# Swin blocks on one core: the subtraction of row maxima as four 32-row products, behind the four biases

## The chip, the cores and the metric

The kernel runs on one core of a Trainium2 chip. Time is that of the device, in microseconds (us), from the start of the program to its end; a profiled execution also gives its span, from the first to the last instruction. Lower is better. The engines are named as the profile names them: PE (TensorE, matmuls), PEld (its weight loads), DVE (VectorE), ACT (ScalarE), POOL (GpSimd), SP (SyncE, which issues most DMAs).

## What is computed

The input is 16 images of 28x28 pixels with 64 channels. Two Swin blocks are applied (the second with windows shifted by 3 and a mask), then a whitening of the channels in groups of 16. What the change touches is the attention in each 7x7 window, for 8 heads of 8 channels:

```
wins = y.reshape(Bn, Hh // WS, WS, Ww // WS, WS, Cc)          # windows of 49 tokens
wins = wins.transpose(0, 1, 3, 2, 4, 5).reshape(-1, N, Cc)
qkv = (wins @ qkv_w + qkv_b).reshape(-1, N, 3, HEADS, hd).transpose(2, 0, 3, 1, 4)
q, k, v = (qkv[0], qkv[1], qkv[2])
attn = jnp.einsum('whnd,whmd->whnm', q, k) * hd ** (-0.5)
attn = attn + bias[None]
attn = attn.reshape(Bn, NW, HEADS, N, N) + mask[None, :, None]
attn = jax.nn.softmax(attn.reshape(-1, HEADS, N, N), axis=-1)
out = jnp.einsum('whnm,whmd->whnd', attn, v)
```

## The kernel before

**Tiling.** An image pair (one image in partitions 0 to 63, one in 64 to 127) is cut into two items of 392 tokens, 8 windows each. A block has 16 items (`HALVES`), and the loop over them is software-pipelined by hand: each engine has its own `step(...)`, written out in the order in which it is to run, and semaphores tie the engines together. Around the two loops of 16 steps stand a start (input, weights, tables), an MLP part behind each block, and the whitening at the end.

**Scores twice.** The softmax needs the row maximum of each query, but the exponential is taken on transposed scores (keys in partitions), where a row maximum lies along partitions. So PE computes the scores of an item twice. `scores` (line 1070) writes them with queries in partitions: a bias product per bank (`bn`), then the products `kexp,qsb`. DVE takes the maxima from there (`rowmax`, line 808, negated, into `nmax`). `split_max` multiplies them by a mask for even and odd windows (`nmaxw`), `maxt` on PE turns them (50 columns, 128 rows in PSUM: one row per combination of window and head), and `spread_max` on DVE writes `rx`, in which each of these 128 rows stands at the columns of its own window and head half only (constant `slot`). One item later `scores_t` (line 1085) writes the transposed scores. They lie in four PSUM banks (`SC`, one bank for each head number h4 = 0..3 within a half), and each of the two groups (`grp`, four windows) fills all four banks: for each bank a bias product (`bt`, 117 rows), then a product of `rx` with a selector (`sel_r`, 128 rows) that adds the negated maximum of the right head to every key; then the products `qexp,ksb`, 16 of 32 rows and 49 columns, each of which the profile counts as two instructions. All in F32R or F32. ACT takes the exponential of two banks at a time (`expo`, line 531), `pv` multiplies with the values, and the row sums go through DRAM to be inverted and spread (`dpk`, `rpk`, `dens`, `rec`).

**Order on PE in a step G** (line 1123 on): `scores_t(G, 0)`, `pv(G-1, 1)`, `f_v`, `scores(G+1, 0)`, two centring products (`xh`, `xl`), `proj(G-2)`, `scores(G+1, 1)`, variance and `f_qk` (`wk`, `wq`) of later items, `scores_t(G, 1)`, `maxt(G+1)`, `pv(G, 0)`.

**What frees the banks.** All score products share the four banks. Before its bias, a group waits for the engine that last read banks 0 and 1, and before the third bias for banks 2 and 3: ACT's exponential (`exp_done`) in the first group of a step, DVE's maxima (`max_done`) in the second. The first group also waits for `rx` (`rx_done`), ahead of everything.

**DVE in a step**: the reciprocals of item G-1, between them the maxima of `scores(G+1, 0)`, the residual, the maxima of `scores(G+1, 1)`, `split_max`, then a chain of eight small operations (`root`, lines 787 to 796, an inverse square root), in the middle of which `spread_max` stands.

**SP in a step**: `dpk` of the second half, `dens` and `rec` of both halves, four transfers `kexp`, four `qexp` for item G+2, and `dpk` of the first half of G, in this order in one queue.

**Start.** ACT's queue loads constants, weights and, as the last large one, the selector `sel` (`sel_f` lies in the memory of `hid`), while SP's queue loads the images. DVE rounds `sel_f` to `sel_r`.

Of the kernel before, what the change touches and what calls it, by code (L numbers as in the profile page):

```python
# [5 lines left out]
F32R = mybir.dt.float32r  # L6
I32 = mybir.dt.int32
ACT = mybir.ActivationFunctionType
ALU = mybir.AluOpType
AX = mybir.AxisListType  # L10

IMAGES, SIDE, CH, HEADS, WS, SHIFT = 16, 28, 64, 8, 7, 3
HD = CH // HEADS
NTOK = WS * WS
# [3 lines left out]
WIN = 2 * WROW  # L18
TOK = WIN * NTOK
IMG_TOK = SIDE * SIDE  # L20
KROWS = 64 + NTOK
# [19 lines left out]
TILES4 = 4  # L41
GWIN = WIN // 2
BANK = GWIN * 2 * NTOK
# [17 lines left out]
def build(nc, x, par, gamma, beta, con, out):  # L61

    ctx = ExitStack()
    with ctx:
        def sb(name, shape, dt=F32):
            return ctx.enter_context(nc.sbuf_tensor(name, shape, dt))
# [30 lines left out]
        wmask = con_view("wmask", KROWS)  # L97
        slot = con_view("slot")
# [8 lines left out]
        hidb = sb("hid", [128, 4, TOK])  # L107

        hid = [hidb[:].rearrange("p (c r) n -> p c r n", c=2), ptb[:, 0].rearrange("p (c r) n -> p c r n", c=2)]
        sel_f = hidb[:].rearrange("p a b -> p (a b)")[:, 0:WIN * 128]  # L110
        sel_r = sb("sel_r", [128, WIN, 128], F32R)


        G1, B1, G2, B2, QB, KB, VB, PB, F2B, FB = 0, 1, 2, 3, 4, 5, 6, 7, 8, 9
# [31 lines left out]
        qsb = sb("qsb", [128, TOK])  # L146
        ksb = [sb(f"ksb{i}", [128, TOK]) for i in range(3)]
        vbd = [sb(f"vbd{i}", [KROWS, WIN * HEADS, 32]) for i in range(2)]
        nmax = sb("nmax", [KROWS, WIN, HEADS])
        nmaxw = sb("nmaxw", [KROWS, WIN // 2, 2, 2 * HEADS], F32R)  # L150
        rx = sb("rx", [128, 2 * GWIN, NTOK], F32R)
        pt = [ptb[0:KROWS, i] for i in range(2)]
        osb = [sb(f"osb{i}", [128, 4 * NROWS]) for i in range(2)]
# [36 lines left out]
        SC = psum[:, 0:TILES4]  # L190
# [485 lines left out]
        def _(dve):  # L676
# [131 lines left out]
            def rowmax(g1, grp):  # L808
                dve.wait_ge(s_ready, 2 * g1 + grp + 1)
                for b in (0, 2):  # L810
                    nc.vector.tensor_reduce(  # L811
                        nmax[:, GWIN * grp:GWIN * grp + GWIN, :].rearrange("p w (g a) -> p a w g", g=2)[:, b:b + 2],
                        SC[0:KROWS, b:b + 2, 0:BANK].rearrange("p a (w g m) -> p a w g m", w=GWIN, g=2),
                        AX.X, ALU.max, negate=True).then_inc(max_done, 1)

            def split_max(g1):

                dve.wait_ge(max_done, 4 * (g1 + 1))
                dve.wait_ge(mxt_ready, g1)
                for w in range(2):  # L820
                    nc.vector.tensor_scalar(nmaxw[:, :, w, :], nmax[:, :, :].rearrange("p (x w) h -> p x (w h)", w=2), wmask[:, w:w + 1], None, ALU.mult)\  # L821
                        .then_inc(nmaxw_done, 1)

            def spread_max(g1):
# [196 lines left out]
        def _(pe):  # L1021
            def mm(o, a, b, start=True, stop=True, **k):
                return nc.tensor.matmul(o, a, b, start=start, stop=stop, **k)  # L1023
# [60 lines left out]

            def scores_t(p, blk, odd, g, grp, buf, pair, free=None):

                if grp == 0:
                    pe.wait_ge(rx_done, g + 1)
                for h4 in range(TILES4):
                    if free and h4 % 2 == 0:  # L1090
                        pe.wait_ge(*free(h4 // 2))
                    mm(SC[0:KROWS, h4, 0:BANK], rows_r[0:BIASR, 0:KROWS], bias_of(p, "bt", blk, odd, grp, h4), True, False)
                    mm(SC[0:KROWS, h4, 0:BANK], sel_r[:, TILES4 * grp + h4, 0:KROWS],
                       rx[:, :, :].rearrange("p s n -> p (s n)"), False, False)
                if grp == 0:
                    pe.wait_ge(qexp_in[buf], 64 * (PAIRS * blk + pair + 1))
                head_scores(ksb[g % 3], qexp[buf], grp).then_inc(st_ready, 1)
# [360 lines left out]
def constants():  # L1458

    import numpy as np  # L1460
    f = np.float32
    pw, pc = np.divmod(np.arange(128), CH)
    same_w = (pw[:, None] == pw[None, :])
    c = {}
    c["ident"] = np.eye(128, dtype=f)
    c["centre"] = (np.eye(128) - same_w / CH).astype(f)
    c["avg64"] = (same_w / CH).astype(f)
    c["avg32"] = ((pw[:, None] == np.arange(64)[None] // 32) / CH).astype(f)
    wide = np.zeros((128, 128), f)
    for c0 in range(2):  # L1470
        for w in range(2):
            wide[64 * c0 + 32 * w, 64 * w:64 * w + 64] = 1
    c["wide"] = wide
    c["dup"] = (pc[:, None] == pc[None, :]).astype(f)
    c["gsum"] = (same_w & (pc[:, None] // GROUP == pc[None, :] // GROUP)).astype(f)
    nw, nn = np.divmod(np.arange(NROWS), NTOK)
    fold = np.zeros((KROWS, 50), f)
    fold[64 * nw + nn, nn] = 1
    c["fold"] = fold
    turn = np.zeros((NTOK, BIASR), f)  # L1480
    turn[NTOK - 1 - nn, 64 * nw + nn] = 1
    both = np.zeros((NTOK, BIASR), f)
    both[nn, 64 * nw + nn] = 1
    c["turn"], c["both"] = turn, both
    c["nmask"] = ((np.arange(128)[:, None] % 32 // 16 == np.arange(2)[None]) & (np.arange(128)[:, None] % 16 < HD)).astype(f)
    for hh in range(2):
        pm = np.zeros((128, 128), f)
        for p in range(128):
            h, dd = divmod(pc[p], HD)
            if h // 4 == hh:  # L1490
                pm[p, 32 * (h % 4) + 16 * pw[p] + dd] = 1
        c[f"perm{hh}"] = pm
    wm = np.zeros((KROWS, 2), f)
    wm[64 * nw + nn, nw] = 1
    c["wmask"] = wm

    pair, rest = np.divmod(np.arange(128), 4 * HEADS)
    odd, rest = np.divmod(rest, 2 * HEADS)
    rw, rh = np.divmod(rest, HEADS)
    at = np.arange(2 * GWIN)  # L1500
    c["slot"] = (4 * (pair[:, None] % 2) + 2 * rw[:, None] + rh[:, None] // TILES4 == at).astype(f)
    sel = np.zeros((128, 2 * TILES4, 128), f)
    for p in range(128):
        sel[p, TILES4 * (pair[p] // 2) + rh[p] % TILES4, 64 * odd[p]:64 * odd[p] + NTOK] = 1

    r, q = np.divmod(np.arange(NTOK), WS)
    low, right = r >= WS - SHIFT, q >= WS - SHIFT
    row = low[:, None] != low[None]
    rows = np.zeros((128, 128), f)
    maskn = np.zeros((BIASR, 4, NTOK), f)  # L1510
    for w in range(2):
        for o in range(2):
            rows[64 * w + np.arange(NTOK), 64 * o + np.arange(NTOK)] = 1
        maskn[64 * w:64 * w + NTOK, 2:] = -100 * row[:, None, :]
        for k in range(4):
            at = 64 * w + NTOK + k
            rows[at, 64 + np.arange(NTOK)] = (low == k // 2) & (right == k % 2)
            maskn[at, 1] = -100 * (right != k % 2)
            maskn[at, 3] = -100 * ((low == k // 2) & (right != k % 2))
    c["rows"] = rows  # L1520
    maskt = maskn
    c["maskn"], c["maskt"] = maskn.reshape(BIASR, -1), maskt.reshape(BIASR, -1)
    packed = np.zeros((128, CON_COLS), f)
    for name, (lo, n) in CON_AT.items():
        packed[0:c[name].shape[0], lo:lo + n] = c[name]
    return {"all": packed, "sel": sel.reshape(128, WIN * 128)}


# [41 lines left out]
```

## Time and profile before

| what | value |
|---|---|
| three runs | 790.99, 793.70, 795.72 us (median 793.7) |
| profiled execution | 792.93 us |
| its span | 791.1 us |
| PE busy, and its share | 711.6 us, 90% |
| DVE busy | 530.8 us, 67% |
| ACT busy | 357.8 us, 45% |
| POOL busy | 204.2 us, 26% |
| `rx,sel_r` products | 256, 88.2 us busy, 344 ns of one |
| `bt,rows_r` products | 256, 101.2 us busy, 395 ns of one |
| row maxima (line 811) | 128, 118.4 us busy, 967 ns of one |
| exponentials (line 531) | 128, 98.6 us busy, 824 ns of one |

The durations of matmuls on PE contain their way through the array; products overlap, and what one costs in a row of equals is the distance from its start to the next start. In the timeline a row with a count (x4) stands for several instructions from the first start to the last end. Shapes are rows*columns of the weights, then partitions x elements. PEld are the weight loads that go with the products.

### The profile page before, as it was taken

Reading aid. Unit: us, or ns where it says so; the run is one execution under the profiler, and the core shown is the slowest. Engines: PE = TensorE matmul, PEld = TensorE weight load, DVE = VectorE, ACT = ScalarE, POOL = GpSimd, SP = SyncE. Lnnn points to the kernel's source line nnn. Section 1 sums busy time; section 2 is a strip of 40 time slices with the busy share of each in tenths; the row PEclk is TensorE's granted clock in tenths of the full one; section 3 lists DMA queues with packets and bytes.
Section 4 is the critical chain, followed back from the end, with each engine's and each line's share of the span. In section 5 each row is a group of like instructions: output and inputs, shape, how many; then the busy total and the mean of one; then the engine's idle time right before and its main releaser. Section 6 shows DMA issues by size and latency. Waiting matters only on the chain. (4 is left out here: it accounts for less than half of the span.)

```text
span 791.1 us, 27074 instructions
## 1 busy us (share of the span) xinstructions
PE 711.6 (90%) x11574; PEld 452.6 (57%) x11574; DVE 530.8 (67%) x919; ACT 357.8 (45%) x628; POOL 204.2 (26%) x505
## 2 busy tenths in 40 slices
PE   3775999999999998899768999999999987999778
PEld 2633567667666765343235677667667653444557
DVE  1644698788778765787545887788888466783123
ACT  2422445455544544675333455445544545664200
POOL 4000022123122111346500123123122114798000
PEclk9967899999999999999967999999999999999859
DMA  9200012112122111000000112112112111000004
GB/s 242 47 20 21 29 58 71 48 57 75 51 63 68 51 57 37 23 1 1 21 21 23 57 60 65 48 58 69 53 56 72 53 36 35 2 1 1 2 20 143
DMA packets 47629, 37.97 MB, mean 48 GB/s; under 512 B 28565, under 2 KB 46997, under 8 KB 47509
## 3 DMA queue, kind: packets, MB, share of 16 engines
q1 hardware_dynamic: 46496, 33.96, 14.9%
q10 hardware_dynamic: 1012, 2.27, 0.9%
q8 instruction: 92, 1.51, 0.8%
q14 instruction: 29, 0.23, 0.1%
HBM read 18.54 MB, written 4.01 MB: 29 GB/s over the span
## 5 line engine op out<-in xcount | busy, mean ns | idle before, releaser
L422 POOL TENSOR_TENSOR att<-osb,rec 128x392 f32<-128x392 f32 x64 | 70.3, 1099 | 374.4 <-DMA rec<-dens 374.4
L811 DVE TENSOR_REDUCE nmax<-psum 113x16 f32<-113x784 f32 x128 | 118.4, 967 | 55.2 <-PE psum L1023 55.0
L531 ACT ACTIVATE pt<-psum 113x784 f32<-113x784 f32 x128 | 98.6, 824 | 105.8 <-PE psum L1023 105.8
L1023 PE MATMUL psum<-bt,rows_r 117*113 117x392 f32 x256 | 101.2, 395 | 2.9 <-DVE rx L827 1.8
L1023 PE MATMUL psum<-rx,sel_r 128*113 128x392 f32 x256 | 88.2, 344 | 0.0
L1023 PE MATMUL psum<-pt,vbd 113*32 113x49 f32 x4096 | 59.8, 209 | 3.3 <-ACT osb L538 3.3
L837 DVE RECIPROCAL rpk<-dpk 64x49 f32<-64x49 f32 x64 | 29.0, 452 | 49.9 <-DMA dpk<-osb 49.6
L1023 PE MATMUL psum<-kexp,qsb 32*49 32x196 f32 x2048 | 60.7, 345 | 0.7 <-DMA kexp<-ksb 0.7
L415 POOL TENSOR_TENSOR xl<-XW,xh 128x392 fp32r<-128x392 f32 x24 | 31.8, 1323 | 113.2 <-ACT xh L498 113.2
L490 ACT ACTIVATE lv<-psum,epsc 128x392 f32<-128x392 f32 x32 | 18.8, 588 | 91.7 <-PE psum L1023 90.6
L1023 PEld LDWEIGHTS psum<-pt,vbd 113*32 113x32 f32 x4096 | 50.7, 110 | 15.0 <-issue 13.8
L1023 PE MATMUL psum<-qexp,ksb 32*49 32x196 f32 x2048 | 58.0, 332 | 0.0
L382 POOL TENSOR_TENSOR XW<-XW,wcol 128x49 f32<-128x49 f32 (+5 forms) x200 | 55.4, 314 | 8.9 <-DVE XW L910 8.7
L1023 PEld LDWEIGHTS psum<-bt,rows_r 117*113 117x113 f32 x256 | 46.0, 180 | 15.7 <-DVE rx L827 3.2
L1023 PE MATMUL psum<-att,wph 128*64 128x196 f32 x512 | 49.5, 334 | 3.2 <-DVE XW L910 2.9
L1023 PE MATMUL psum<-bn,rows_r 53*113 53x392 f32 x256 | 44.0, 409 | 7.6 <-DVE nmax L811 7.4
L1023 PEld LDWEIGHTS psum<-rx,sel_r 128*113 128x113 f32 x256 | 46.1, 180 | 5.3 <-issue 4.6
L1023 PE MATMUL psum<-sq,conb 128*128 128x392 f32 (+1 forms) x96 | 46.5, 568 | 2.3 <-ACT sq L484 2.3
L1023 PEld LDWEIGHTS psum<-kexp,qsb 32*49 32x49 f32 x2048 | 35.1, 121 | 19.2 <-issue 17.2
L364 POOL COPY XW<-XW 128x64 f32<-128x64 f32 (+2 forms) x192 | 37.4, 255 | 27.9 <-DVE XW L910 27.9
L1023 PEld LDWEIGHTS psum<-att,wph 128*64 128x64 f32 x512 | 33.4, 135 | 19.3 <-issue 8.8
L787 DVE TENSOR_SCALAR ly<-lv 128x392 int32<-128x392 int32 x48 | 20.1, 419 | 36.2 <-ACT lv L490 30.6
(174 smaller groups left out, 1254.0 us busy)
## 6 DMA issues: line engine op xcount, KB each, us to landing
rec<-dens SPq DMA_DIRECT2D x64, 196.0 KB
kexp<-ksb SPq DMA_DIRECT2D x128, 49.0 KB
qexp<-qsb SPq DMA_DIRECT2D x128, 49.0 KB
XW<-x_dram SPq DMA_DIRECT2D x14, 196.0 KB, 4.6
out_dram<-XW SPq DMA_DIRECT2D x14, 196.0 KB, 2.4
dpk<-osb SPq DMA_DIRECT2D x64, 12.2 KB
dens<-rpk SPq DMA_DIRECT2D x64, 12.2 KB, 2.6
pt<-w_dram ACTq DMA_DIRECT2D x2, 384.0 KB, 6.9
```

The lines of the kernel that those rows point to most:

```text
L364: last = nc.gpsimd.tensor_copy(dst[:, i, jo:jo + jn, ro:ro + rn, co:co + cn], src[:, si, ji:ji + jn, ri:ri + rn, ci:ci + cn])
L382: last = nc.gpsimd.tensor_tensor(dst[:, y0:y0 + rn, q0:q0 + cn], src[:, i, j, r0:r0 + rn, c0:c0 + cn], wcol[:, SHIFTC:SHIFTC + 1].rearrang ...
L415: nc.gpsimd.tensor_tensor(xl[:, :], xcols(blk, g + AHEAD), xh[:, :].bitcast(F32), ALU.subtract)\
L422: nc.gpsimd.tensor_tensor(att[:, 4 * part:4 * part + 4, :], osb[part][:, :].rearrange("p (a n) -> p a n", a=4), rec[part][:, :].rearrange( ...
L490: nc.scalar.activation(lv[buf][:, :], bB[:, 0:TOK], ACT.Identity, bias=epsc[:, 0:1]).then_inc(var_used, 1)
L531: nc.scalar.activation(pt[grp][:, b:b + 2, :], SC[0:KROWS, b:b + 2, 0:BANK], ACT.Exp)\
L787: ln(nc.vector.tensor_scalar(ly[:, :].bitcast(I32), v[:, :].bitcast(I32), -0.5, MAGIC, ALU.mult, ALU.add))
L811: nc.vector.tensor_reduce(nmax[:, GWIN * grp:GWIN * grp + GWIN, :].rearrange("p w (g a) -> p a w g", g=2)[:, b:b + 2], SC[0:KROWS, b:b + 2 ...
L837: nc.vector.reciprocal(rpk[part][:, :], dpk[part][:, :]).then_inc(rec_done, 1)
L1023: return nc.tensor.matmul(o, a, b, start=start, stop=stop, **k)
```

## The change

1. `nmax` is laid out by bank (h4) first, and so the turned maxima come in the order h4, group, window pair, odd, rw, half. The 32 rows from 32*h4 on hold all that bank h4 needs, for both groups.
2. The selector is only 2 x 128 columns for each row (one for each group) in place of 8 x 128. The product of bank h4 takes only rows 32*h4 to 32*h4 + 31 of `sel_r` and of `rx`.
3. In `scores_t` the four biases come first, then the wait for `rx` (first group only), then the four subtractions, each in other rows of the array and in another bank, then `qexp,ksb` as before.
4. The constants `slot` and `sel` follow the new order; `sel` in DRAM is 128 x 256 in place of 128 x 1024.

```diff
-        sel_f = hidb[:].rearrange("p a b -> p (a b)")[:, 0:WIN * 128]
-        sel_r = sb("sel_r", [128, WIN, 128], F32R)
+        sel_f = hidb[:].rearrange("p a b -> p (a b)")[:, 0:2 * 128]
+        sel_r = sb("sel_r", [128, 2, 128], F32R)
...
-        nmax = sb("nmax", [KROWS, WIN, HEADS])
-        nmaxw = sb("nmaxw", [KROWS, WIN // 2, 2, 2 * HEADS], F32R)
+
+        nmax = sb("nmax", [KROWS, TILES4, 2, 2 * GWIN])
+        nmaxw = sb("nmaxw", [KROWS, 4 * TILES4, 2, TILES4], F32R)
...
                     nc.vector.tensor_reduce(
-                        nmax[:, GWIN * grp:GWIN * grp + GWIN, :].rearrange("p w (g a) -> p a w g", g=2)[:, b:b + 2],
-                        SC[0:KROWS, b:b + 2, 0:BANK].rearrange("p a (w g m) -> p a w g m", w=GWIN, g=2),
+                        nmax[:, b:b + 2, grp, :],
+                        SC[0:KROWS, b:b + 2, 0:BANK].rearrange("p a (k m) -> p a k m", m=NTOK),
...
             def scores_t(p, blk, odd, g, grp, buf, pair, free=None):
 
-                if grp == 0:
-                    pe.wait_ge(rx_done, g + 1)
                 for h4 in range(TILES4):
                     if free and h4 % 2 == 0:
                         pe.wait_ge(*free(h4 // 2))
                     mm(SC[0:KROWS, h4, 0:BANK], rows_r[0:BIASR, 0:KROWS], bias_of(p, "bt", blk, odd, grp, h4), True, False)
-                    mm(SC[0:KROWS, h4, 0:BANK], sel_r[:, TILES4 * grp + h4, 0:KROWS],
-                       rx[:, :, :].rearrange("p s n -> p (s n)"), False, False)
+                if grp == 0:
+                    pe.wait_ge(rx_done, g + 1)
+                for h4 in range(TILES4):
+                    r = slice(32 * h4, 32 * h4 + 32)
+                    mm(SC[0:KROWS, h4, 0:BANK], sel_r[r, grp, 0:KROWS], rx[r, :, :].rearrange("p s n -> p (s n)"), False, False)
```

On PE, the second group of a step (`z,wq` is `f_qk`, `qexp,ksb` the transposed scores), before:

```order
L1023 MATMUL psum<-z,wq 128x392 [waits var_used]
L1023 MATMUL psum<-bt,rows_r 113x392 [waits max_done]
L1023 MATMUL psum<-rx,sel_r 113x392
L1023 MATMUL psum<-bt,rows_r 113x392
L1023 MATMUL psum<-rx,sel_r 113x392
L1023 MATMUL psum<-bt,rows_r 113x392 [waits max_done]
L1023 MATMUL psum<-rx,sel_r 113x392
L1023 MATMUL psum<-bt,rows_r 113x392
L1023 MATMUL psum<-rx,sel_r 113x392
L1023 MATMUL psum<-qexp,ksb 49x196 x16
```

The same place on PE after the change:

```order
L1024 MATMUL psum<-z,wq 128x392 [waits var_used]
L1024 MATMUL psum<-bt,rows_r 113x392 [waits max_done]
L1024 MATMUL psum<-bt,rows_r 113x392
L1024 MATMUL psum<-bt,rows_r 113x392 [waits max_done]
L1024 MATMUL psum<-bt,rows_r 113x392
L1024 MATMUL psum<-rx,sel_r 113x392 x4
L1024 MATMUL psum<-qexp,ksb 49x196 x16
```

The subtractions left the places between the biases; only one product now stands between the two waits for the maxima.

On PE, the first group of a step, behind `pv` of the step before (`pt,vbd`), before:

```order
L1023 MATMUL psum<-pt,vbd 32x49 x31
L1023 MATMUL psum<-bt,rows_r 113x392 [waits exp_done,rx_done]
L1023 MATMUL psum<-rx,sel_r 113x392
L1023 MATMUL psum<-bt,rows_r 113x392
L1023 MATMUL psum<-rx,sel_r 113x392
L1023 MATMUL psum<-bt,rows_r 113x392 [waits exp_done]
L1023 MATMUL psum<-rx,sel_r 113x392
L1023 MATMUL psum<-bt,rows_r 113x392
L1023 MATMUL psum<-rx,sel_r 113x392
L1023 MATMUL psum<-qexp,ksb 49x196 [waits qexp_in1]
```

And after:

```order
L1024 MATMUL psum<-pt,vbd 32x49 x31
L1024 MATMUL psum<-bt,rows_r 113x392 [waits exp_done]
L1024 MATMUL psum<-bt,rows_r 113x392
L1024 MATMUL psum<-bt,rows_r 113x392 [waits exp_done]
L1024 MATMUL psum<-bt,rows_r 113x392
L1024 MATMUL psum<-rx,sel_r 113x392 [waits rx_done]
L1024 MATMUL psum<-rx,sel_r 113x392 x3
L1024 MATMUL psum<-qexp,ksb 49x196 [waits qexp_in1]
```

The wait for `rx` went behind the biases, and the second wait for the exponential is one product, no longer three, behind the first bias.

## Rows read from the trace of the kernel before

**Rows 1.** The page: busy time of PE, and its granted clock in 40 slices

```profile
PE 711.6 (90%) x11574; PEld 452.6 (57%) x11574; DVE 530.8 (67%) x919; ACT 357.8 (45%) x628; POOL 204.2 (26%) x505
...
PEclk9967899999999999999967999999999999999859
```

**Rows 2.** Table by stretches: length, busy PE, PEld, DVE, ACT, POOL, clock, DMA

```profile
150.00:210.00 60.00, 59.89 (x1285) 41.26 (x1284) 49.57 (x76) 30.35 (x53) 15.26 (x14) 1.00 0.20 61
```

**Rows 3.** Timeline of PE, second group of a step: start, us, instruction, idle before

```profile
160.17 0.93 PE L1023 MATMUL psum<-z,wq 128*128 128x392 f32 x2
160.63 0.64 PE L1023 MATMUL psum<-bt,rows_r 117*113 117x392 f32 x1
161.12 0.34 PE L1023 MATMUL psum<-rx,sel_r 128*113 128x392 f32 x1
...
162.22 0.34 PE L1023 MATMUL psum<-rx,sel_r 128*113 128x392 f32 x1
162.48 0.91 PE L1023 MATMUL psum<-qexp,ksb 32*49 32x196 f32 x32
```

**Rows 4.** Timeline of PE, the first group of the next step

```profile
164.47 0.41 PE L1023 MATMUL psum<-bt,rows_r 117*113 117x392 f32 x1
...
165.25 0.34 PE L1023 MATMUL psum<-bt,rows_r 117*113 117x392 f32 x1
...
166.07 0.91 PE L1023 MATMUL psum<-qexp,ksb 32*49 32x196 f32 x32
```

**Rows 5.** Timelines there of PE's weight loads (third bias) and of ACT

```profile
165.09 0.18 PEld L1023 LDWEIGHTS psum<-bt,rows_r 117*113 117x113 f32 x1
...
163.50 1.54 ACT L531 ACTIVATE pt<-psum 113x784 f32<-113x784 f32 x2 [1.35 <-PE psum L1023]
```

**Rows 6.** Timeline of PE, `scores`: biases in two rounds, then `kexp`

```profile
153.77 0.61 PE L1023 MATMUL psum<-bn,rows_r 53*113 53x392 f32 x4
154.04 0.34 PE L1023 MATMUL psum<-bn,rows_r 53*113 53x392 f32 x2
154.31 0.41 PE L1023 MATMUL psum<-kexp,qsb 32*49 32x196 f32 x8
```

**Rows 7.** Timelines of DVE and SP over one turn; DVE's wait, 430 to 620

```profile
170.46 1.86 DVE L811 TENSOR_REDUCE nmax<-psum 113x16 f32<-113x784 f32 x2 [1.26 <-PE psum L1023]
...
185.11 0.46 DVE L837 RECIPROCAL rpk<-dpk 64x49 f32<-64x49 f32 x1 [1.46 <-DMA dpk<-osb]
185.49 1.84 DVE L811 TENSOR_REDUCE nmax<-psum 113x16 f32<-113x784 f32 x2
...
172.71 0.51 SPq L308 DMA_DIRECT2D dens<-rpk  x1
176.57 0.60 SPq L315 DMA_DIRECT2D rec<-dens  x1
...
183.25 0.65 SPq L300 DMA_DIRECT2D dpk<-osb  x1
...
DVE rpk L837 <- DMA dpk<-osb: 14.3, 12, 2.7
```

**Rows 8.** The start: timeline of PE, DMA issue of `sel`, DMA traffic 6:12

```profile
11.34 1.54 PE L1213 MATMUL psum<-conb,XW 112*128 112x112 f32 x7 [11.34 <-DMA XW<-x_dram]
...
hid<-c_sel_dram ACTq DMA_DIRECT2D x1, 512.0 KB, 8.6
...
DMA packets 2685, 1.87 MB, mean 312 GB/s; under 512 B 2302, under 2 KB 2302, under 8 KB 2685
```

**Rows 9.** Timelines at the end of the first block: PE, ACT, DVE

```profile
300.10 0.44 PE L1023 MATMUL psum<-bt,rows_r 117*113 117x392 f32 x1 [0.90 <-DVE rx L827]
...
301.73 0.91 PE L1023 MATMUL psum<-qexp,ksb 32*49 32x196 f32 x32
...
298.24 1.54 ACT L531 ACTIVATE pt<-psum 113x784 f32<-113x784 f32 x2 [2.50 <-PE psum L1023]
...
299.48 0.56 DVE L827 TENSOR_TENSOR rx<-psum,conb 128x392 fp32r<-128x392 f32 x1
```

More of the change, by code:

```diff
@@ L820, in split_max @@
                 for w in range(2):
-                    nc.vector.tensor_scalar(nmaxw[:, :, w, :], nmax[:, :, :].rearrange("p (x w) h -> p x (w h)", w=2), wmask[:, w:w + 1], None, ALU.mult)\
+                    nc.vector.tensor_scalar(nmaxw[:, :, w, :], nmax[:, :, :, :].rearrange("p a x (y k) -> p (a x y) k", y=2), wmask[:, w:w + 1], None, ALU.mult)\
                         .then_inc(nmaxw_done, 1)
@@ L1495, in constants @@
     c["wmask"] = wm
[L1497 to L1502, printed above, removed]
+    _, group, pair, odd, rw, hg = np.unravel_index(np.arange(128), (TILES4, 2, 2, 2, 2, 2))
+    c["slot"] = (4 * pair[:, None] + 2 * rw[:, None] + hg[:, None] == np.arange(2 * GWIN)).astype(f)
+    sel = np.zeros((128, 2, 128), f)
     for p in range(128):
-        sel[p, TILES4 * (pair[p] // 2) + rh[p] % TILES4, 64 * odd[p]:64 * odd[p] + NTOK] = 1
+        sel[p, group[p], 64 * odd[p]:64 * odd[p] + NTOK] = 1
     r, q = np.divmod(np.arange(NTOK), WS)
@@ L1525, in constants @@
         packed[0:c[name].shape[0], lo:lo + n] = c[name]
-    return {"all": packed, "sel": sel.reshape(128, WIN * 128)}
+    return {"all": packed, "sel": sel.reshape(128, 2 * 128)}
 def kernel(**inputs):
```

## The prediction

> **What bounds the kernel now.** Read the page first: PE is busy 90% of the span, and its clock row shows 2.4 GHz (9 tenths) but for the start and the stretch near 400 us [rows 1]. Then the table by stretches: inside a block, 150 to 210 us, PE is busy 59.89 of 60 us at clock 1.00 [rows 2]. So a microsecond taken off PE's path there counts, until something else ends last. The changed products stand at two places of each step, and the timeline of PE is read at both. One step is about 15.0 us; there are 16 in each of two blocks.
>
> *Second group* (windows 4 to 7 of the item). The first bias starts at 160.63, while the second pass of `wq` still runs (0.49 us to the next product), and from `rx` at 161.12 to `rx` at 162.22 six products follow 0.18 us apart, until `qexp` takes over at 162.48: 1.85 us [rows 3]. Nothing is waited for: this is PE's own time.
>
> *First group.* It takes 1.60 us, 164.47 to 166.07 [rows 4]. But look at the third bias, which needs banks 2 and 3. Its weight load starts at 165.09, and the second half of ACT's exponential ends at 163.50 + 1.54 = 165.04 [rows 5]. The third bias starts as soon as ACT has emptied its banks. That exponential in turn starts when the second group before it is finished. So from one group's `qexp` (162.48) to the third bias of the next (165.25) the path runs through ACT, and a faster PE does not shorten it. The two subtractions that PE does between the biases now fill a time in which it would wait.
>
> **The change part by part.**
> *Four banks side by side.* The nearest row is `bn`: four products of 53 rows go in two rounds, two at a time, 153.77 and 154.04, and the next shape starts at 154.31, 0.27 after the second [rows 6]. Products in different row groups run together there, and `kexp` shows eight starts within its first 0.41 us [rows 6]. From these rows: a change of shape costs 0.27 instead of 0.18 from the last product's start to the next one, as `sel_r` to `qexp` does now (162.22 to 162.48, [rows 3]), and the first round after it shows 0.09 more (0.27 instead of 0.18), its weight load, which nothing covers. One round of four, with a shape change behind it, is then 0.27 + 0.09 = 0.36 us. Below it lies 0.27 (the load hidden), above it 0.54 (two rounds, as `bn`). I take 0.36, since no row shows more than one round for products in different row groups.
>
> *Second group*: 0.48 to the second bias, 0.18 twice, 0.27 for the change from 128 rows to 32, 0.36 for the round: 1.48 against 1.85, a gain of 0.37 (0.19 to 0.46). The biases' own waits on the row maxima do not come to bear, since PE still has `wq` before them.
>
> *First group*: from the third bias on, before 0.82 (165.25 to 166.07 [rows 4]), after 0.18 + 0.27 + 0.36 = 0.81. Gain 0.01 (a loss of 0.17 to a gain of 0.10). What was taken from in front of the third bias turns into waiting for ACT. The wait for `rx` moved behind four biases costs nothing here: `rx` is long written by then.
>
> The Trainium skill speaks against the change at one point: "TensorEngine Tiling (Array Packing)", Key Properties, says that a change of the tiling mode drains the engine, and the change adds one such change to every group. Rows 3 and 6 agree, with 0.27 instead of 0.18. The page "TensorE: Matmul & The Clock Gate", Measured speedup vs the span model, gives 3.07 times for four row tiles, not 4; by that, as an estimate, a round would last about a third longer, some 0.06 us, and the sum would be some 2 us smaller.
>
> *What takes over when the step is shorter.* A second loop runs beside PE's: reciprocal on DVE, `dens` and `rec` on the SP queue, then the eight spreads of the next item, then `dpk`, then the reciprocal that stands on DVE in front of the step's first row maximum. In one step it goes 172.71 (`dens`), 176.57 (`rec`), 183.25 (`dpk`), 185.11 (reciprocal), and the maximum follows at 185.49 with no idle time, where the step before, at 170.46, had 1.26 us to spare: 15.03 us round [rows 7]. That step has nothing to give. I went through the 26 turns from one step's first maximum to the next. In 15 DVE waits 0.38 us or more for PE before that maximum (as at 170.46), so the full 0.37 is gained. In the other 11, the reciprocal's DMA, or in one step the DVE's table work, leaves less (as at 185.49); together they give 0.6 us. In the second block DVE waited 12 times for `dpk`, 14.3 us in all [rows 7]. Steady steps: 15 x 0.37 + 0.6 = 6.2 us.
>
> *The opening of each block* has two groups that end nothing but PE's own row (ACT has no exponential before them, or one long done): 4 x 0.37 = 1.5 us.
>
> *The end of each block.* At 300.10 the first group waited 0.90 us for `rx` (299.48 + 0.56); the exponential had ended at 298.24 + 1.54 = 299.78 [rows 9]. Now the biases run during that wait: third at 299.84, fourth 0.27 later, subtractions at 300.38, `qexp` at 300.74 instead of 301.73. That is 1.0 us, twice: 2.0 us. The exponential, the DMA of `osb` and the tail behind it start from there. The bound below is 0.4 each, should a release on ACT or SP come late.
>
> *The smaller constant.* `sel` shrinks from 512 KB to 128 KB. PE's first product waits until 11.34 for the first image, whose packets share the engines with `sel` (it lands 8.6 us after its issue), at a mean of 312 GB/s [rows 8]. 384 KB less is 1.26 us of that traffic. The image is not behind `sel` in one queue but beside it, so the gain lies between 0 and 1.26; I take 1.0, since all engines were full until the image was there. All that follows in the start hangs on that image. The shorter cast of `sel_r` on DVE lies beside PE's transposes and counts nothing.
>
> The maxima in another order are the same instructions on the same number of elements: nothing gained or lost.
>
> *Sum*: 1.0 + 1.5 + 6.2 + 2.0 = 10.7 us. The profiled execution took 792.93 us (span 791.1), so 782.2. The median of the three runs, 793.7, is 0.8 above it; I say **782.5**.
>
> **The rivals.**
> *Two rounds.* Four banks written at full rate may come out two at a time; for it, `bn` is the only row at this rate and has two. Then a group costs 0.18 more: 0.19 gained in the second, 0.17 lost in the first, nothing in a steady step; 1.0 for the start, about 0.8 for the openings, 1.6 for the ends: 789.5.
> *One by one, slower than before.* If the 113 output columns keep the four from running together, they cost 0.18 each behind an additional shape change: 0.36 + 3 x 0.18 = 0.90 for the four. From the third bias on the first group then takes 0.18 + 0.27 + 0.90 = 1.35 instead of 0.82, and the second gains -0.17: 0.7 us lost in each of 26 turns, 18 us, with the start's gain 810. It decides from the point at which the round costs more than 0.54. Against it: `kexp` and `bn` run together.
> *The reciprocal's DMA loop takes nearly all.* It needs landings of `dens` as late as the one at 176.57 in most steps; the step would stay near 15 us and only start, openings and ends count with some 1.5 us of the rest: 787.
> *More than forecast.* Between subtraction and `qexp` the rows of a tile stay 32; if that change costs nothing and the load is hidden, the round is 0.18: the second group gains 0.55, the first 0.19. Half of the turns can take it: 778.
>
> **How the numbers follow.** Forecast 0.70 (780 to 786), two rounds 0.07, one by one 0.05, the DMA loop 0.09, more 0.09. The range leaves out the slower rival and little else: 776 to 789.5. A measurement of this kernel can tell about 0.5% from no change, 4 us, so faster means under 789.7: forecast, DMA loop, more and half of the two rounds, less a little for what I have not thought of: 0.89 faster, 0.05 same, 0.06 slower.
>
> **What would show it.** Four `rx,sel_r` products of 32 rows starting within some 0.03 us, `qexp` 0.36 behind them; a second group of about 1.48 us; in the first group the third bias right behind the exponential's second half, and the group still about 1.60 us; steps of 14.7 us with some of 15.0 where `nmax` has no idle time before it; a first product near 10.3 us. Wrong would be: a round of over 0.5 us, a first image that comes no earlier, `dpk` waits in nearly every step, or a first group that no longer waits for ACT.

## The result, and the profile after

The changed kernel takes 785.59 us (median of 16 runs, 779.37 to 791.86) against 794.87 for the kernel before on the same chips (16 runs, 787.89 to 799.81). The ratio is 0.9892, with a 95% interval of 0.9867 to 0.9916: 8.6 us faster. (The ratio leaves out slow runs, those more than 1.5% above the fastest of their kernel, one on each side; the medians of all sixteen lie 9.3 us apart.) Two later series of the changed kernel gave 0.9906 and 0.9876. The forecast was 782.5 from 793.7, a ratio of 0.986: the sign and most of the size came true, and 0.986 lies just outside the measured interval. The profiled execution has a span of 780.8 us, against 791.1.

The page and the table by stretches, to be read against [rows 1] and [rows 2] (columns: length, busy us of PE, PEld, DVE, ACT, POOL, granted clock, DMA share, GB/s):

```profile
PE 693.6 (89%) x11574; PEld 414.3 (53%) x11574; DVE 534.0 (68%) x919; ACT 357.8 (46%) x628; POOL 205.0 (26%) x505
...
PEclk9866999999999999999978999999999998999859
```

```profile
150.00:210.00 60.00, 59.07 (x1306) 37.23 (x1300) 50.84 (x77) 30.41 (x52) 15.44 (x13) 1.00 0.20 61
```

PE is busy 18.0 us less in all, but the time fell by about 10. In the stretch of [rows 2] PE is no longer busy to the last tenth: it idles 0.93 of 60 us. Part of what the products gave back has turned into waiting.

The same step as in [rows 3] and [rows 4], on PE's timeline, then ACT's exponential before the first group, then PE's load of its third and fourth bias (start, us, instruction, idle before):

```profile
159.67 1.19 PE L1024 MATMUL psum<-bt,rows_r 117*113 117x392 f32 x4
160.79 0.43 PE L1024 MATMUL psum<-rx,sel_r 32*113 32x392 f32 x4
161.15 0.91 PE L1024 MATMUL psum<-qexp,ksb 32*49 32x196 f32 x32
...
163.06 1.32 PE L1024 MATMUL psum<-bt,rows_r 117*113 117x392 f32 x4
164.31 0.43 PE L1024 MATMUL psum<-rx,sel_r 32*113 32x392 f32 x4
164.67 0.91 PE L1024 MATMUL psum<-qexp,ksb 32*49 32x196 f32 x32
```

```profile
162.17 1.54 ACT L532 ACTIVATE pt<-psum 113x784 f32<-113x784 f32 x2 [0.99 <-PE psum L1024]
```

```profile
163.76 0.27 PEld L1024 LDWEIGHTS psum<-bt,rows_r 117*113 117x113 f32 x2 [0.42 <-ACT pt L532]
```

- The four subtractions fill one line of 0.43 us, and `qexp` starts 0.36 us after their first (160.79 to 161.15): the forecast's round of four, to the hundredth.
- The second group takes 159.67 to 161.15, 1.48 us (forecast 1.48, before 1.85).
- The first group takes 163.06 to 164.67, 1.61 us (forecast about 1.60). Its third bias is loaded at 163.76, 0.05 after the exponential's end (162.17 + 1.54 = 163.71), and the row names ACT for the 0.42 us before it.

The end of the first block, against [rows 9]:

```profile
295.76 1.32 PE L1024 MATMUL psum<-bt,rows_r 117*113 117x392 f32 x4
297.01 0.43 PE L1024 MATMUL psum<-rx,sel_r 32*113 32x392 f32 x4
297.38 0.91 PE L1024 MATMUL psum<-qexp,ksb 32*49 32x196 f32 x32
```

The 0.90 us in front of the first bias are gone. The first group there was 301.73 - 300.10 = 1.63 us long behind that wait, 2.53 with it; now it is 1.62.

What was *not* as forecast is on DVE and SP. First DVE's waits between 430 and 620 (us in all, times, longest), then the latest turn of the second block, as DVE and as SP show it:

```profile
DVE rpk L838 <- DMA dpk<-osb: 18.0, 11, 6.3
DVE nmax L812 <- PE psum L1024: 13.5, 19, 1.3
```

```profile
561.53 0.46 DVE L838 RECIPROCAL rpk<-dpk 64x49 f32<-64x49 f32 x1 [3.30 <-DMA dpk<-osb]
561.91 1.78 DVE L812 TENSOR_REDUCE nmax<-psum 113x16 f32<-113x784 f32 x2
```

```profile
551.38 0.61 SPq L316 DMA_DIRECT2D rec<-dens  x1
552.09 3.75 SPq L286 DMA_DIRECT2D kexp<-ksb  x4
555.93 3.64 SPq L294 DMA_DIRECT2D qexp<-qsb  x4
559.67 1.39 SPq L301 DMA_DIRECT2D dpk<-osb  x2
```

```profile
562.87 0.43 PE L1024 MATMUL psum<-bn,rows_r 53*113 53x392 f32 x2 [1.41 <-DVE nmax L812]
```

Read from the bottom. PE waits 1.41 us for a row maximum (and then again). The maximum stands on DVE behind the reciprocal, and the reciprocal stood idle 3.30 us for `dpk`. SP issued that gather at 559.67 only, since the eight spreads of K and q come first on its queue and their issue took 552.09 to 559.57. This turn lasted 16.75 us instead of 14.57. One of 17.16 stands in the first block. A *turn* is counted here from the first bias of one second group to that of the next step; the experiments below use the 21 steady ones (10 in the first block, 11 in the second), and call late what is over the usual turn by more than 0.1 us (the last column adds up what lies above the usual turn plus 0.03).

| | usual turn | late of 21 | us over the usual turn, in all |
|---|---|---|---|
| before | 15.02 | 4 | 1.3 |
| changed, first profile | 14.57 | 7 | 6.9 |
| changed, second | 14.57 | 8 | 7.8 |
| changed, third | 14.57 | 12 | 13.5 |

### The profile page after: what moved, and what is told of

The parts are those of the page before. It is cut to its first block and busy times, and to the rows that moved or that the text cites. A ratio compares the mean times of both kernels' runs of the same rounds, so it can differ in the third digit from the quotient of the medians.

```text
span 780.8 us, 27044 instructions
## 1 busy us (share of the span) xinstructions
PE 693.6 (89%) x11574; PEld 414.3 (53%) x11574; DVE 534.0 (68%) x919; ACT 357.8 (46%) x628; POOL 205.0 (26%) x505
## 3 DMA queue, kind: packets, MB, share of 16 engines
q8 instruction: 91, 1.49, 0.8%
## 5 line engine op out<-in xcount | busy, mean ns | idle before, releaser
L1024 PE MATMUL psum<-bt,rows_r 117*113 117x392 f32 x256 | 79.0, 409 | 3.9 <-DVE nmax L812 1.2
L383 POOL TENSOR_TENSOR XW<-XW,wcol 128x49 f32<-128x49 f32 (+5 forms) x200 | 55.3, 314 | 11.8 <-DVE XW L911 11.6
L1024 PEld LDWEIGHTS psum<-bt,rows_r 117*113 117x113 f32 x256 | 40.9, 180 | 29.9 <-ACT pt L532 12.7
L1024 PEld LDWEIGHTS psum<-kexp,qsb 32*49 32x49 f32 x2048 | 34.9, 120 | 18.2 <-issue 16.4
L796 DVE SCALAR_TENSOR_TENSOR lt<-lt,lv 128x392 f32<-128x392 f32 x48 | 40.6, 846 | 1.6
L1024 PEld LDWEIGHTS psum<-qexp,ksb 32*49 32x49 f32 x2048 | 34.2, 117 | 12.4 <-issue 12.1
```

The lines of the kernel that those rows point to most:

```text
L383: last = nc.gpsimd.tensor_tensor(dst[:, y0:y0 + rn, q0:q0 + cn], src[:, i, j, r0:r0 + rn, c0:c0 + cn], wcol[:, SHIFTC:SHIFTC + 1].rearrang ...
L796: ln(nc.vector.scalar_tensor_tensor(lt[:, :], lt[:, :], -0.5 * THIRD ** 3, v[:, :], ALU.mult, ALU.mult))
```

## Experiments on the round of four

**The order alone, with 128 rows.** The kernel before, with its eight selector matrices and its order of maxima, but with the four biases first and then the four subtractions:

```
     for h4 in range(TILES4):
         mm(SC[0:KROWS, h4, 0:BANK], rows_r[0:BIASR, 0:KROWS], bias_of(...), True, False)
-        mm(SC[0:KROWS, h4, 0:BANK], sel_r[:, TILES4 * grp + h4, 0:KROWS], rx[...], False, False)
+    if grp == 0:
+        pe.wait_ge(rx_done, g + 1)
+    for h4 in range(TILES4):
+        mm(SC[0:KROWS, h4, 0:BANK], sel_r[:, TILES4 * grp + h4, 0:KROWS], rx[...], False, False)
```

> The kernel before with the new order alone: the four biases of a group first, then the four subtractions, each still of 128 rows (the maxima stay ordered as before and the selector has its eight matrices). So the products stand where the change puts them, and nothing runs side by side. My theory, that the gain is four products at a time: a second group takes 1.85 us as before (no gain), the first group starts its subtractions behind the third bias, which waits for the exponential's end at 0.65 us behind the group's start, and then owes four of 0.17 to 0.18 us where before it owed two, so a step of 15.04 becomes 15.3 to 15.4 where TensorE sets it; with the two block ends better by 0.3 to 0.7 each (the biases before the wait for the maxima), the whole is 3 to 8 us slower than the kernel before, ratio 1.004 to 1.010. The rival, that it is the new place of the wait for the maxima that brings the gain: 0.99 to 1.00.

Measured: 1.0035 of the kernel before (1.0010 to 1.0061), slower, just under the range I gave. On PE's timeline:

```profile
437.53 1.19 PE L1023 MATMUL psum<-bt,rows_r 117*113 117x392 f32 x4
438.55 0.87 PE L1023 MATMUL psum<-rx,sel_r 128*113 128x392 f32 x4
439.36 0.91 PE L1023 MATMUL psum<-qexp,ksb 32*49 32x196 f32 x32
...
441.27 1.31 PE L1023 MATMUL psum<-bt,rows_r 117*113 117x392 f32 x4
442.41 0.88 PE L1023 MATMUL psum<-rx,sel_r 128*113 128x392 f32 x4
443.22 0.41 PE L1023 MATMUL psum<-qexp,ksb 32*49 32x196 f32 x8
```

The second group is 1.83 us, as before. The first is 1.95, since all four subtractions now come behind the third bias's wait, and the usual turn 15.27 instead of 15.02. So the new order by itself costs 0.25 us a turn. It is not what gains; that the 32-row products need it is shown by the run after the next.

**32 rows, but one block of rows for all.** The changed kernel, with all four products on rows 0 to 31 (three of the four banks subtract other heads' maxima):

```
-                    r = slice(32 * h4, 32 * h4 + 32)
+                    r = slice(0, 32)
```

> The changed kernel with its order and its 32-row products, but all four of a group take rows 0 to 31 (so three of the four banks are given the maxima of the wrong heads): four small products one behind the other on one block of rows. If the gain is that four blocks of rows work side by side, the round of four rises from 0.37 us by three times the 0.18 us that one product takes behind another, to 0.9, a second group from 1.48 to 2.0, a turn from 14.57 to 15.65, and the time to 816 us or so, 1.03 of the kernel before. If small products are cheap by themselves, or the gain is the order alone, it stays at 0.989.

Measured: 1.0127 (1.0089 to 1.0164).

```profile
446.02 1.19 PE L1024 MATMUL psum<-bt,rows_r 117*113 117x392 f32 x4
447.13 0.96 PE L1024 MATMUL psum<-rx,sel_r 32*113 32x392 f32 x4
448.02 0.91 PE L1024 MATMUL psum<-qexp,ksb 32*49 32x196 f32 x32
```

The round takes 0.89 us (447.13 to 448.02) instead of 0.36, the second group 2.00, the usual turn 15.62: the forecast's price for "one by one" (0.90), and within 0.03 of what was expected of the turn. The four blocks of rows are the gain. The whole came out 8 us under the 816 expected, for a reason that bears on the rest: of its 21 turns none was late. I had added the turn's difference to a kernel that loses 7 to 13 us to late turns, and at 15.62 there are none to lose.

**32 rows, one behind each bias.** The changed kernel with bias and subtraction in turn, as the kernel before has them:

```
     for h4 in range(TILES4):
         mm(..., bias_of(...), True, False)
+        r = slice(32 * h4, 32 * h4 + 32)
+        mm(SC[0:KROWS, h4, 0:BANK], sel_r[r, grp, 0:KROWS], rx[r, :, :]..., False, False)
```

> The changed kernel with its 32-row products, but each one right behind its own bias, as the kernel before has them: bias, subtraction, bias, subtraction. Two products of 32 rows never stand next to each other, so nothing runs side by side, and the shape changes at each one. My theory (concurrency gives the gain, and a change of shape costs the 0.09 to 0.1 us that the round of four holds beyond its streaming): a second group becomes 1.85 to 2.6 us, so steps of 15.1 to 16.1, and the time 795 to 822, ratio 1.00 to 1.035, with 1.03 as the value of the sum (0.18 per product more than side by side, four per group and two groups, 32 turns). The rival, that 32 rows are cheap by themselves: the second group at 1.5 to 1.6 and a ratio of 0.99.

Measured: 1.1043 (1.0991 to 1.1095), 881 us. The direction holds, the size is far outside what I gave. First PE, then PEld:

```profile
163.48 0.44 PE L1024 MATMUL psum<-bt,rows_r 117*113 117x392 f32 x1
163.85 0.42 PE L1024 MATMUL psum<-rx,sel_r 32*113 32x392 f32 x1
164.20 0.43 PE L1024 MATMUL psum<-bt,rows_r 117*113 117x392 f32 x1
```

```profile
163.48 0.17 PEld L1024 LDWEIGHTS psum<-bt,rows_r 117*113 117x113 f32 x1 [0.19 <-issue]
163.84 0.17 PEld L1024 LDWEIGHTS psum<-rx,sel_r 32*113 32x113 f32 x1 [0.20 <-issue]
```

Every product, the biases too, starts 0.36 us after the one before, where in [rows 3] it is 0.18. The weight load of 0.17 us starts together with its product instead of beneath the previous one. A product between two changes of shape costs its load and its stream, twice the price. I had charged this to the subtractions and forgot the biases. The sum then closes: a group has nine changes of shape instead of three, 6 x 0.18, and three products that no longer run beside the first, 3 x 0.18, make 1.62 us. The second group went from 1.48 to 3.09 (162.55 to 165.64), 1.61 more.

**The constant's size.** The changed kernel, with `sel` transferred as 512 KB again (the added part is zeros and unused), and the changed kernel itself beside it:

```
-    return {"all": packed, "sel": sel.reshape(128, 2 * 128)}
+    return {"all": packed, "sel": np.concatenate([sel.reshape(128, 2 * 128), np.zeros((128, 6 * 128), f)], 1)}
```

> The changed kernel, with one part undone: the selector's transfer is again 512 KB (the part behind the first 128 KB is zeros and is not used). My theory: the smaller constant is worth 384 KB at the 312 GB/s of the start, up to 1.2 us, though the first product of the two traces moved by 0.16 us alone (11.34 to 11.18), so this kernel should be 0.2 to 1.3 us slower than the changed one, 0.9905 of the kernel before. The rival: the load is hidden at the start and nothing is lost (0.9892 of the kernel before). In both cases nearly all of the 8.6 us must still be there; if the ratio rises above 0.994, the gain lay in the start and not in the products.

> The changed kernel itself, on the chip of the three others, as their yardstick: 0.9892 of the kernel before, from 0.987 to 0.992; the profile should again show a round of four at 0.37 us, a second group of 1.49 us, and, of the 30 steady turns, about half held by the reciprocals' gather rather than by TensorE.

Measured: 0.9887 (0.9839 to 0.9935) with the large constant, 0.9906 (0.9874 to 0.9938) for the changed kernel on that chip. The times don't separate them. The profiles of these two, large first, do:

```profile
11.38 0.98 PE L1215 MATMUL psum<-conb,XW 112*128 112x112 f32 x4 [11.38 <-DMA XW<-x_dram]
```

```profile
10.49 1.54 PE L1215 MATMUL psum<-conb,XW 112*128 112x112 f32 x7 [10.49 <-DMA XW<-x_dram]
```

One pair could be chance, but every kernel of this study begins alike. In the five profiles with 512 KB the first product comes at 11.15 to 12.01, 11.54 on the mean ([rows 8] is one); in the eight with 128 KB at 10.20 to 11.18, 10.67 on the mean (the first profile of the changed kernel is the latest of them). The small constant is worth 0.9 us at the first product. That the whole time falls by as much is not shown, and nothing of the rest hangs on it.

## Experiments on what was given back

**The gather earlier on SP's queue.** Both kernels, with SP issuing `dpk` ahead of the four spreads of q instead of behind them:

```
                     if G + 2 < base + HALVES:
                         spread_k(G + 2)
-                        spread_q(G + 2)
                     gather(G, 0)
+                    if G + 2 < base + HALVES:
+                        spread_q(G + 2)
```

> The kernel before with one move on SyncE's queue: the gather of the next turn's sums (dpk from osb) is issued between the copies of K and those of q, so ahead of the four q copies instead of behind them. Nothing else is changed. My theory: the gather, and VectorE's reciprocal that waits for it, hold only some of the 26 steady turns of the kernel before (those above 15.04 us), so it gains 1 to 2 us, ratio 0.997 to 0.999. The rival, that turns come late for another reason (TensorE's own, or a transfer that collides with another): no change or slower by up to 2 us, because the q copies now land later.

> The changed kernel with the same move on SyncE's queue (the gather of the sums ahead of the four q copies). The steady turns of the changed kernel are 14.56 where TensorE sets them, but in its two profiles turns of 14.8 to 17.2 stand among them, 8 to 9 us in all over 14.57. My theory: these are turns that the gather and the reciprocal hold, and with the gather issued earlier nearly all become 14.57: 4 to 8 us under the changed kernel, ratio 0.981 to 0.986 of the kernel before. The rival, that the lateness is not the place of the gather on the queue but its landing time itself, or the q copies: no change against the changed kernel, ratio 0.989 to 0.991.

Measured: 0.9958 (0.9928 to 0.9989) for the kernel before, 0.9772 (0.9733 to 0.9811) for the changed one. Both gained more than I had given (0.997 to 0.999 and 0.981 to 0.986). The changed kernel takes 776.19 us, 17.5 below the kernel before on that chip. DVE's waits of the changed kernel with the move, 430 to 620, and SP at the place of the late turn above:

```profile
DVE nmax L813 <- PE psum L1025: 26.3, 25, 2.1
DVE rpk L839 <- DMA dpk<-osb: 5.4, 3, 3.5
```

```profile
546.48 2.41 SPq L286 DMA_DIRECT2D kexp<-ksb  x4
549.17 1.07 SPq L301 DMA_DIRECT2D dpk<-osb  x1
550.34 2.38 SPq L294 DMA_DIRECT2D qexp<-qsb  x4
```

The gather lands while DVE still works on its tables, DVE waits 3 times for it instead of 11, and before 25 row maxima DVE waits for PE: PE sets the time again. Two of the 21 turns are late, by 0.5 us in all. In the kernel before there was little to remove (1.3 us late, 1.2 with the move), and yet it gained 3.3 us by the ratio. The 21 turns don't show where that comes from (they sum to 316.9 and 316.6 us), and the interval reaches down to 0.9 us. Of the 3.6 us between the two profiles, 1.5 are there at the first group of all (65.58 against 64.09) and 1.7 arise between the first two groups of block 2 (20.18 against 18.52); the kernel with the order alone, which has no move, is as short in both places (61.36 and 18.41). So the profiles don't tie this gain to the move.

A second measurement stood beside the changed kernel on one chip:

> The changed kernel with the gather of the sums ahead of the four q copies, a second time, beside the changed kernel itself on one chip: 0.974 to 0.981 of the kernel before, and 12 to 14 us under the changed kernel if the first measurement holds, 6 to 9 if only the late turns that the two profiles of the changed kernel show (8 to 9 us over 14.57 per turn) go.

> The changed kernel, on the chip of the two others: 0.987 to 0.992 of the kernel before, with late turns among those of 14.57 as in its two other profiles.

0.9751 (0.9725 to 0.9776) against 0.9876 (0.9841 to 0.9911): 777.38 against 787.72 us, 10.3 us for moving one issue. The profiles have 1.2 and 13.5 us of late turns. It is between the two cases I had written down. This is the best of the kernels measured that leave nothing out.

With the move on both sides, the change is worth 0.9772 / 0.9958 = 0.981, or 14 to 15 us (the medians are 790.28 and 776.19), instead of 8.6.

**Half an exponential.** As above, and ACT's exponential of each second group takes half of its columns (the other half is left out; the first item of a block keeps it whole):

```
+                n = BANK // 2 if grp and g % HALVES else BANK
...
-                    nc.scalar.activation(pt[grp][:, b:b + 2, :], SC[0:KROWS, b:b + 2, 0:BANK], ACT.Exp)
+                    nc.scalar.activation(pt[grp][:, b:b + 2, 0:n], SC[0:KROWS, b:b + 2, 0:n], ACT.Exp)
```

> The move of the kernel two above, and ScalarE's exponential of each second group takes only half of its columns (but for the first item of each block); the other half is left out. In the kernel before, the first group has bias, subtraction, bias, subtraction, and the third bias waits for that exponential's end 0.65 us behind the group's start, while TensorE reaches it at about the same time. Expected: the exponential costs TensorE little here, 0 to 0.35 us of a turn of 15.04, so steady turns of 14.7 to 15.04 and a time 0 to 9 us under the same kernel with the whole exponential.

> The changed kernel with the same move and the same half exponential (half of the second group's columns left out). My theory of the first group: its four biases want 0.75 us and stand 0.42 longer, because the third waits for the exponential's end at 0.65; without that wait the first group takes 1.28 as at the openings of the blocks' last groups instead of 1.61, so turns of 14.57 become 14.24, and the time is 8 to 10 us under the same kernel with the whole exponential. The rival, that the first group's length is TensorE's own (the load of the 32-row weights or a drain): turns stay at 14.5 to 14.6 and the time within 2 us.

Measured: 0.9949 (0.9921 to 0.9977) for the kernel before, against 0.9958 with the whole exponential: no difference that the intervals can tell. 0.9698 (0.9646 to 0.9750) for the changed kernel, against 0.9772: 770.16 us, 6.0 less. PE and ACT of the changed kernel:

```profile
444.81 0.98 PE L1026 MATMUL psum<-bt,rows_r 117*113 117x392 f32 x4
445.71 0.43 PE L1026 MATMUL psum<-rx,sel_r 32*113 32x392 f32 x4
446.08 0.91 PE L1026 MATMUL psum<-qexp,ksb 32*49 32x196 f32 x32
```

```profile
443.91 0.89 ACT L534 ACTIVATE pt<-psum 113x392 f32<-113x392 f32 x2 [0.99 <-PE psum L1026]
```

The exponential ends at 444.80, before the first bias, and the first group falls from 1.61 to 1.27 us. The usual turn is 14.24 instead of 14.57; in the kernel before it goes from 15.01 to 14.96. So ACT's exponential costs the changed kernel 0.33 us in each turn and cost the kernel before 0.05. The turn is as expected; the time fell by 6.0 where I had said 8 to 10, because I had counted 30 turns, not 21. The 21 fell from 306.7 to 300.2 us in all, 6.5; outside them the first groups are shorter too (1.28 us), but the turns are not.

## Why the prediction was right, and where it was not

**The round of four and the second group: right.** 0.36 and 1.48 us, as forecast from `bn` and from the change `sel_r` to `qexp` [rows 3, 6]. A control shows the rival's price too: 0.89 on one block of rows, forecast 0.90. The kernel that alternates, at 0.36 instead of 0.18 us a product, agrees with the rule of the Trainium skill, "TensorEngine Tiling (Array Packing)", Key Properties, that a change of the tiling mode drains the engine. A lone 32-row product between two changes takes 0.36 (163.85 to 164.20 is 0.35), and so do four side by side. So the third that I had weighed by the Trainium skill, "TensorE: Matmul & The Clock Gate", Measured speedup vs the span model, doesn't show: by it the round would have been about 0.42, an estimate. Against the four on one block of rows (0.89) the round is 2.5 times as fast, not four times, since the 0.18 us around them stay.

**The first group: right in kind, short in size.** I gave it 0.01 us. It waits for ACT, as said, and the half exponential shows the price. But the usual turn fell from 15.02 to 14.57, 0.45, of which the second group is 0.37. The remaining 0.08 lies on the path through ACT: from the end of the exponential to `qexp` it was 1.03 (165.04 to 166.07 [rows 4, 5]) and is 0.96 (163.71 to 164.67). The term that was mis-sized is the 0.18 from the third bias to the fourth. From the third bias's load I had 0.16 to its product and 0.18 to the next, 0.34; in the changed kernel the loads of both stand in one row of 0.27 us, and the fourth product starts 0.27 behind the third's load. The kernel before has the same at the head of this group, behind `pt,vbd`: its first two loads start 0.09 apart (164.44 and 164.53), where those inside the group are 0.18 apart. I had taken the distance from inside the group, though after the change PE's loads stand idle before the third bias too. Why the second of two loads follows so closely there, no row says.

**The steady steps: the mechanism named, its term mis-sized.** I gave them 6.2 us: 15 turns with 0.37, and 11 in which the loop of `dens`, `rec`, spreads and `dpk` leaves 0.6 together. The 21 turns sum to 316.86 us in the kernel before (mean 15.09) and to 313.15 in the first profile of the changed one (mean 14.91): 3.7 us. In its second profile it is 2.8, and the third has a mean of 15.23, no gain at all. By the usual turn it should be 21 x 0.45 = 9.5. The forecast's sum was for 26 turns, so those have to be set against it (taken here from second group to second group, 84.89 to 280.00 and 425.67 to 621.06 before): they gave 5.0 us in the first profile of the changed kernel, 3.2 in the second and -2.2 in the third, 2.0 on the mean, for 6.2 forecast. The step that failed is that the slack was read turn by turn from a kernel that ran at 15.0: where DVE had 0.38 us to spare, I let the turn have its gain in full. But the loop has its own length and its own late landings, and by the order of SP's queue it can carry lateness on, since the spreads stand behind `rec` and `dpk` stands behind the spreads (argued; no run isolates it). Late turns were 1.3 us at 15.02 and 6.9 to 13.5 at 14.57, and none at 15.62. The rival "the DMA loop takes nearly all" had 0.09; for the steady turns alone it was nearer to what happened, on the mean of the three profiles, than the forecast (1.5 us against 6.2, with 2.0 measured), and its 787 is also nearer to the 785.6 measured than 782.5 is. Its mechanism, a step that stays near 15 us, did not come: the usual turn is 14.57, and the loss is in few and long turns.

**The openings: right.** 1.5 us forecast for two groups of each block. From first bias to `qexp` they took 2.43 and 1.84 us in the first block and 3.07 and 1.84 in the second; now they take 2.22, 1.49, 2.57 and 1.48: 1.4 us less.

**The ends of the blocks: right.** From the first bias of the last first group back to that of the second group before it, the path is unchanged, and the wait for `rx` is gone from the front: 1.0 at the first block's end (295.76 where the kernel before had 300.10, 4.34 earlier, when the second group before it, at 292.07 where it had 295.43, was 3.36 earlier). The second block shows the same, 11.76 to 12.78. The forecast had no term for the very last group of each block (306.58 to 308.21 before, 302.22 to 303.50 now, 0.35 shorter) nor for the turn behind the 26 (0.4 in each block).

**The start: right on the mean.** 1.0 forecast from 1.26 us of traffic; 0.2 in the first profile of the changed kernel, 0.9 over all thirteen profiles. One profile of each would have called the term wrong.

**Why the whole fits nevertheless.** The first profile of the changed kernel, against that of before, at the first biases of marked groups:

| place | before | changed | gain so far | of it here |
|---|---|---|---|---|
| first product | 11.34 | 11.18 | 0.2 | 0.2 |
| first group of all | 65.58 | 63.22 | 2.4 | 2.2 |
| block 1, 26 turns begin | 84.89 | 82.43 | 2.5 | 0.1 |
| block 1, second group before the last first group | 295.43 | 292.07 | 3.4 | 0.9 |
| block 1, last first group | 300.10 | 295.76 | 4.3 | 1.0 |
| block 2, first group | 405.49 | 400.30 | 5.2 | 0.9 |
| block 2, 26 turns begin | 425.67 | 418.74 | 6.9 | 1.7 |
| block 2, second group before the last first group | 635.88 | 624.12 | 11.8 | 4.8 |
| block 2, last first group | 640.60 | 627.82 | 12.8 | 1.0 |
| end of the span | 791.1 | 780.8 | 10.3 | -2.5 |

(The 26 turns are 13 in each block.) Three of these lines are not the change's, or only in part. The 2.2 us arise between 24 and 34: the products of the start that follow the image's transposes are shorter there in the first profile, and the `sq` products behind them start at 31.46 where the kernel before has 34.07, 2.6 us earlier. (The granted clock reads 1.00 from 24 to 30 in both, so it doesn't tell the difference.) Two of these products show it; in the second profile of the changed kernel they take 1.68 us again, as before, and the first group stands at 64.91, 0.7 earlier than before, not 2.4. First profile, then second:

```profile
29.92 0.96 PE L1024 MATMUL psum<-XW,conb 128*128 128x392 f32 x2
```

```profile
30.95 1.68 PE L1024 MATMUL psum<-XW,conb 128*128 128x392 f32 x2
```

The 1.7 stand in a stretch where the granted clock differs, between the first two groups of block 2. The kernel before and then the changed one:

```profile
405.49:425.67 20.18, 14.34 (x140) 8.22 (x139) 9.39 (x17) 6.20 (x11) 0.00 (x0) 0.68 0.06 20
```

```profile
400.30:418.74 18.44, 12.58 (x140) 6.62 (x139) 8.43 (x13) 6.48 (x11) 0.00 (x0) 0.75 0.07 22
```

The -2.5 stand where PE waits for `wcol` in the last MLP part. The kernel before has its slow products in front of that wait, where they cost little; the changed kernel, whose products in front took their usual time (`z,f` 1.59 us), has them behind it, after a longer idle time, with a granted clock of 0.74 from 648 to 661. Before, then changed:

```profile
655.36 2.55 PE L1023 MATMUL psum<-z,f 64*128 64x392 f32 x8
661.92 0.38 PE L1023 MATMUL psum<-wcol,conb 128*128 128x1 f32 x2 [2.54 <-DVE wcol L935]
662.23 1.59 PE L1023 MATMUL psum<-z,f 64*128 64x392 f32 x8
```

```profile
648.96 0.59 PE L1024 MATMUL psum<-wcol,conb 128*128 128x1 f32 x2 [4.12 <-DVE wcol L936]
649.47 2.98 PE L1024 MATMUL psum<-z,f 64*128 64x392 f32 x8
```

All three places vary from profile to profile, in kernels without the change too. The kernel with the order alone, which has no 32-row product, has its first group at 61.36, and 18.41 us between the first two groups of block 2; the changed kernel with one block of rows for all has 20.13 there. Over all thirteen profiles this stretch takes 18.2 to 20.2 us, and from `wcol` to the end it is 129.0 to 131.9 us.

So the forecast of 10.7 us met 8.6 with errors that partly cancel: the 26 turns brought less than the 6.2 of the sum, since late turns took more, and the first group's 0.08 a turn, the last groups and the turn behind the 26 were not in it. That the sum came this near is in part luck. What places the slow products and the lower clock differently from profile to profile was not tried.

## What to carry to other kernels

Products with few rows are worth putting side by side only if they stand together: four on four blocks of rows cost what one costs (0.36 us), but each of them alone between other shapes costs twice a product in a row, and so does its neighbour. When the engine that sets the time is made faster, look for the next loop at the *new* length of the step, its lateness included, and put the small transfer that someone waits for ahead of the large ones on its queue: here that one line, on the changed kernel, was worth about as much as the change itself (10.3 us, where the change alone brought 9 to 10 on the same chip). An engine's wait that costs 0.05 us a turn can cost 0.33 once the work that covered it is gone.

## What the runs showed of the hardware that I had not expected

- A change between 117 and 32 rows at every product doubles the price of both kinds (0.36 instead of 0.18 us a product), and the load of 0.17 us is no longer beneath the product before it. Over the kernel this is 10% (1.1043), where I had expected 3.5% at most.
- The issue of four spreads of K on SP took 2.43 us in one turn and 3.75 in another of the same profile, with the same instructions. In the late turn above the excess is in one of the four, the third, of K as of q (1.89 and 1.78 us; the third of K takes 0.58 in the next turn), and the program has no wait between them. The eight took 7.4 us there and 7.3 in the late turn of the first block (3.55 and 3.75), and 4.9 to 6.2 in the other turns. Which is cause and which effect stays open.
- A loop of small transfers that shows 1.3 us of lateness in 21 turns of 15.02 shows 6.9 to 13.5 at 14.57 and none at 15.62. It has no one length; its effect grows while the turn comes down to it.
